# Moving the second weight matrix by eight words in both slots of an expert kernel

## The reference

```python
x = x + 0.5 * ffn(layernorm(x), Wr, W1, W3, W2)
x = x + attn(layernorm(x), Wq, Wk, Wv, Wc, Ltri)
x = x + 0.5 * ffn(layernorm(x), Wr, W1, W3, W2)
```

```python
h  = silu(xe @ W1[e]) * (xe @ W3[e])     # [tokens,256] x [256,1024], twice
ye = h @ W2[e]                           # [tokens,1024] x [1024,256]
out[token] += gate * ye
```

## The kernel before, in words

| what | address before | mod 64, mod 512 |
|---|---|---|
| slot A (`c_wa`), W1 high | 29184 | 0, 0 |
| slot A, W1 low | 53760 | 0, 0 |
| slot A, W2 high and low | 45568, 70144 | 0, 0 |
| slot B (`e_wb`), W1 high | 108064 | 32, 32 |
| slot B, W1 low | 132640 | 32, 32 |
| slot B, W2 high and low | 124448, 149024 | 32, 32 |
| `xT` high and low, `h` high and low | 157440, 161536, 173824, 190208 | 0, 256 |

## Time and profile before

### The profile page before, as it was taken

The page is one execution under the profiler, slowest core; times in us unless marked ns, Lnnn a source line. Parts: engine busy times, 40 slices in busy tenths (PEclk is TensorE's granted clock), DMA queues, the critical chain, the costliest instruction groups (busy, mean ns, idle before and its releaser), DMA issues.

```text
span 2968.2 us, 54854 instructions
## 1 busy us (share of the span) xinstructions
PE 2831.0 (95%) x18723; PEld 2535.6 (85%) x18723; DVE 1606.7 (54%) x3765; ACT 1305.6 (44%) x2765; POOL 1164.9 (39%) x1550
## 2 busy tenths in 40 slices
PE   4499999999999999989999995999999999999999
PEld 3389899989999989878888885998999998899988
DVE  8754545455454545447878875444545454545453
ACT  5543434444344434334444444444434343444443
POOL 3754434444444434310111113453444443444533
PEclk8799999999999999999999997999999999999999
DMA  7552323232332312121121014223323231323212
GB/s 247 194 127 36 80 36 79 43 78 39 84 63 54 86 31 42 33 59 33 57 70 47 31 45 123 57 43 76 83 38 79 41 86 29 81 42 79 43 29 34
DMA packets 155114, 197.23 MB, mean 66 GB/s; under 512 B 15536, under 2 KB 127024, under 8 KB 154928
## 3 DMA queue, kind: packets, MB, share of 16 engines
q0 software_dynamic: 62688, 87.11, 17.9%
q1 hardware_dynamic: 81952, 97.30, 10.1%
q10 hardware_dynamic: 10288, 10.38, 1.0%
HBM read 124.32 MB, written 78.79 MB: 68 GB/s over the span
## 4 chain that ended last, share of the span: by engine, by line
PE 54%; DVE 1%; ACT 0%; issue 0%; DMA 0%; POOL 0%; DVEq 0%; ACTq 0%; POOLq 0%
PE e_ps L100 8%; PE e_ps L102 8%; PE e_ps L101 8%; PE e_psy L1198 5%; PE mi_qk L1453 4%; PE e_ps L1198 3%; PE e_psy L1200 3%; PE mi_sc L1469 2%; PE mi_yo L1489 2%; PE mi_xv L1459 2%; PE mi_yo L1516 2%; PE e_ps L1200 2%; PE mi_kv L1503 1%; PE e_psx L1184 1%; PE mi_yo L1477 1%; PE mi_qk L1510 0%
## 5 line engine op out<-in xcount | busy, mean ns | idle before, releaser
L1301 DVE TENSOR_TENSOR e_h_lo<-e_hid,e_h_hi 128x384 fp32r<-128x384 f32 (+1 forms) x640 | 384.2, 600 | 399.3 <-ACT e_h_hi L1262 390.4
L1298 DVE TENSOR_TENSOR e_hid<-e_ps,e_gate 128x384 f32<-128x384 f32 (+1 forms) x640 | 381.9, 597 | 371.8 <-ACT e_gate L1258 357.3
L1262 ACT ACTIVATE e_h_hi<-e_hid 128x384 fp32r<-128x384 f32 (+1 forms) x640 | 356.9, 558 | 424.1 <-DVE e_hid L1298 417.0
L1258 ACT ACTIVATE e_gate<-e_ps 128x384 f32<-128x384 f32 (+1 forms) x640 | 333.8, 522 | 405.3 <-PE e_ps L102 397.9
L100 PE MATMUL e_ps<-e_xT_hi,e_wb 128*128 128x384 f32 (+1 forms) x1280 | 456.3, 357 | 0.0
L101 PE MATMUL e_ps<-e_xT_lo,e_wb 128*128 128x384 f32 (+1 forms) x1280 | 455.0, 355 | 0.0
L102 PE MATMUL e_ps<-e_xT_hi,e_wb 128*128 128x384 f32 (+1 forms) x1280 | 454.9, 355 | 0.0
L100 PE MATMUL e_ps<-e_xT_hi,c_wa 128*128 128x384 f32 (+1 forms) x1280 | 450.5, 352 | 2.5 <-DVE e_xT_lo L1290 2.5
L102 PE MATMUL e_ps<-e_xT_hi,c_wa 128*128 128x384 f32 (+1 forms) x1280 | 448.6, 350 | 0.0
L101 PE MATMUL e_ps<-e_xT_lo,c_wa 128*128 128x384 f32 (+1 forms) x1280 | 448.5, 350 | 0.0
L461 POOL DMA_INDIRECT c_xrow<-normed_rows,e_token x320 | 346.6, 1083 | 153.2 <-POOL e_token L1087 77.9
(11 more groups left out here) (302 smaller groups left out, 4772.3 us busy)
## 6 DMA issues: line engine op xcount, KB each, us to landing
c_raw<-w SPq DMA_DIRECT2D x204, 256.0 KB
normed_rows<-r_xn SPq DMA_DIRECT2D x8, 1056.0 KB, 7.1
normed_rows<-mi_xn SPq DMA_DIRECT2D x8, 1056.0 KB, 4.8
x<-x ACTq DMA_DIRECT2D x8, 1024.0 KB, 12.0
out<-mi_x SPq DMA_DIRECT2D x8, 1024.0 KB, 5.3
r_xin<-x SPq DMA_DIRECT2D x7, 1024.0 KB, 11.0
c_raw<-x SPq DMA_DIRECT2D x7, 1024.0 KB, 8.3
c_xrow<-normed_rows,e_token POOLq DMA_INDIRECT x320
```

The costliest lines, as they stand in the source:

```text
L1258: act.activation(gate[:, f % 2, 0:n], ps1[f % 2][:, 0:n], ACT.Silu).then_inc(gated, 1)
L1262: act.activation(h[0][:, f, 0:n], hid[:, f % 2, 0:n], ACT.Copy).then_inc(h_high, 1)
L1298: dve.tensor_tensor(hid[:, f % 2, 0:n], ps3[f % 2][:, 0:n], gate[:, f % 2, 0:n], ALU.mult).then_inc(hid_ready, 1)
L1301: dve.tensor_tensor(h[1][:, f, 0:n], hid[:, f % 2, 0:n], h[0][:, f, 0:n].bitcast(F32), ALU.subtract).then_inc(h_ready, 1)
```

## The change

Each part of a slot is widened from 6144 to 6160 words (`SPLIT`), and W2's columns begin at 4104 (`W2SPLIT`) in place of 4096. `split_piece` replaces `piece` wherever a piece is written to a slot or read back from it for the low part; the unsplit weights (`raw`) keep their layout. Slot B gets a spacer of 8 words ahead of it and one of 56 words behind it.

```diff
+SHIFT = 8
+W2SPLIT = W2AT + SHIFT
+SPLIT = WCOLS + 2 * SHIFT
...
+def split_piece(t, q):
+
+    at = q * PIECE + (SHIFT if q * PIECE >= W2AT else 0)
+    return t[:, at:at + PIECE]
...
-                    act.activation(piece(slot_a[:, 0], q), piece(raw, q), ACT.Copy).then_inc(w_high, 1)
+                    act.activation(split_piece(slot_a[:, 0], q), piece(raw, q), ACT.Copy).then_inc(w_high, 1)
...
-        slot_b = m.sb("wb", [P, 2, WCOLS], F32R)
+        m.sb("wb_shift", [P, SHIFT])
+        slot_b = m.sb("wb", [P, 2, SPLIT], F32R)
+        m.sb("wb_rest", [P, 7 * SHIFT])
...
-                        at = W2AT + f * D
+                        at = W2SPLIT + f * D
...
-        slot_a = m.sb("wa", [P, 2, WCOLS], F32R)
+        slot_a = m.sb("wa", [P, 2, SPLIT], F32R)
```

More of the change, by code:

```diff
@@ L861, in low_w @@
                     dve.wait_ge(w_high, q + 1)
-                    dve.tensor_tensor(piece(slot_a[:, 1], q), piece(raw, q), piece(slot_a[:, 0], q).bitcast(F32),
+                    dve.tensor_tensor(split_piece(slot_a[:, 1], q), piece(raw, q), split_piece(slot_a[:, 0], q).bitcast(F32),
                                       ALU.subtract).then_inc(w_low, 1)
@@ L908, in _ @@
                             pool.wait_ge(w_high, q + 1)
-                            pool.tensor_tensor(piece(slot_a[:, 1], q), piece(raw, q), piece(slot_a[:, 0], q).bitcast(F32),
+                            pool.tensor_tensor(split_piece(slot_a[:, 1], q), piece(raw, q), split_piece(slot_a[:, 0], q).bitcast(F32),
                                                ALU.subtract).then_inc(w_low, 1)
@@ L1243, in high_w @@
                     wait_raw(act, raw_loaded, e + loaded - 1, q)
-                    act.activation(piece(slots[1 - s][:, 0], q), piece(raw, q), ACT.Copy).then_inc(w_high, 1)
+                    act.activation(split_piece(slots[1 - s][:, 0], q), piece(raw, q), ACT.Copy).then_inc(w_high, 1)
                 def high_x(n, width=WIDE):
@@ L1283, in low_w @@
                     dve.wait_ge(w_high, PIECES * e + q + 1)
-                    dve.tensor_tensor(piece(slots[1 - s][:, 1], q), piece(raw, q), piece(slots[1 - s][:, 0], q).bitcast(F32),
+                    dve.tensor_tensor(split_piece(slots[1 - s][:, 1], q), piece(raw, q), split_piece(slots[1 - s][:, 0], q).bitcast(F32),
                                       ALU.subtract).then_inc(w_low, 1)
```

## The result

The changed kernel takes 2973.50 us (median of 22 runs, 2970.73 to 2975.44) against 2970.06 us of the kernel before in the same rounds (22 runs, 2968.18 to 2973.40). The ratio is 1.0013, 95% interval 1.0007 to 1.0019: slower by 3.4 us, where 13.8 us less had been forecast. The profiled execution has a span of 2971.5 us, 3.3 us more than before.

The account below looks back on a forecast made before the run. TensorE's distance from one matmul's start to the next was taken to bound both expert stages. Savings of 6.2 + 7.6 = 13.8 us, other items 0, took 2971.63 to 2957.8 us; range 2953 to 2973.

Parts of the forecast that it names:

- Items 4, 5 and 6: Slot writes at new remainders, earlier need for gathers, attention tensors moved by 128 bytes: each taken as costing nothing.
- Parts 1 and 2: Slot A's second product takes slot B's price, 6.2 us less; slot B's first product takes slot A's, 7.6 us less.
- No change: Rival: the slots' memory region makes their difference, so the change leaves both as they are; 2971.6 us, chance 0.13.
- Only one of the two: Rival: price depends also on history, so only one part's gain arrives; about 2965 us, chance 0.16.
- item 3: Slot A's W1 and slot B's W2 keep remainders modulo 64: 0 us, bounded by +31 and -31 us.
- item 6: Attention stage: its own tensors move by 128 bytes against constants that stay; taken as 0 us.
- The slower rival: 64 bytes between high and low part make slot A's 512 first and slot B's second products dear; +12.5 us, chance 0.15.

Follow-up runs that it names:

- e3: Kernel before with W2 moved 8 words in slot A only, high and low part at the same remainder: 2962.80 against 2970.00 us, ratio 0.9978.
- e4: Kernel before with only slot B changed, W1 at 0 and W2 at 32 modulo 512, no gap: 2961.75 against 2970.00 us, ratio 0.9973.
- e1: Kernel before with W1 at 0 and W2 at 32 modulo 512 in both slots, no gap between high and low part: 2954.98 against 2970.00 us, ratio 0.9950.
- e10: Changed kernel with slot B's start at 0 modulo 512 in place of 192, 64-byte gap kept: 2969.54 us, ratio 1.0000 to the kernel before.
- e5: e1 with slot B's start at 192 modulo 512, still no gap: 2962.48 us, ratio 0.9976 to the kernel before.
- e11: e1 with both slots starting at 64 modulo 512, xT and h unmoved: 2987.28 us, ratio 1.0058 to the kernel before.
- e12: e11 with xT, gate, hid and h moved by the same 64 bytes: 2955.50 us, ratio 0.9952 to the kernel before.
- e8: e1 with xT moved 8 words, to 32 modulo 64: 2969.47 us, ratio 0.9998 to the kernel before.
- e7: e1 with W2 16 words (64 bytes) behind its old place: 2968.26 us, ratio 0.9996 to the kernel before.

## Why the prediction was wrong

**The bound held.** TensorE's matmul distances set the end in both expert stages, before and after, and nothing became late: the waits have not grown and the attention has not changed. Items 4, 5 and 6 (writes, gathers, attention), costed at nothing, were right.

**Parts 1 and 2 were right in mechanism and size, taken by themselves.** 6.2 and 7.6 us had been forecast; e3 and e4 measured 7.2 and 8.3 us, and e1 15.0 us for both against 13.8. The excess of about 1 us is a price better than either slot had: the first product of 512 tokens takes 21.78 us in both slots of e1 where 21.83 had been forecast, 24 x 0.05 = 1.2 us. "No change" by the region of the memory falls with them: in e3 and e4 a slot takes the other's price without leaving its region. "Only one of the two" falls too, since the two add.

**The step that failed is item 3**, "0 us, if 64 bytes is the length that counts". Put at 0, it measured about +17 us: the changed kernel is 3.4 us slower where the other items gave 13.8 us less. The length is 256 bytes for the gap, and the change moves two things within it: the low part against the high part by 64 bytes, and slot B's start from 32 to 192, not to 0. Both slots being "at 0 modulo 64" was true and meant little. What they cost, in the step's own terms:

- The gap costs 15 us (e1 against e10). In the mean durations it sits on the product with the low part and the one before it (397 and 392 ns against 389).
- Slot B's start at 192 costs 7.5 us when there is no gap (e1 against e5). With the gap it costs less: 4 us by the medians of the runs (changed kernel against e10, with intervals that overlap), 2 us by the tile times summed over the two profiles: against e10, the second product in slot B loses 2.8 us and its 384 first product 1.1 us, and its 512 first product gains 2.3 us. The addresses agree with this smaller price: with a length of 256 bytes, the change puts slot B's low part back at 0 (256 modulo 512), and it is the high part that lies off, by -64. Its 512 first product, 22.02 us, is nearer to e5's 21.99 than to e10's 22.19. The tensors that item 6 speaks of moved by 128 bytes in the changed kernel and not in e10; no run tries that alone, and the attention, where it would show too, has not changed.

So -15 us for the two parts, +15 for the gap and +2 to +4 for slot B's start give about the +3.4 us measured. The upper bound that item 3 gave to itself, +31 us, was wide enough. The choice of 0, "which is where both slots agree for the 384 tiles although their addresses differ", used two remainders, 0 and 32, as if they stood for all. The remainders that the change makes new (64, 192, 224) had no row.

**The slower rival had the mechanism and not the price.** It named the 64 bytes between high and low part, and asked for L102's successor to split from the other two, which it does (397 against 389 ns). It had given +12.5 us, on the assumption that the dear price would replace each good one and that nothing would be gained. In fact the gain of the second product in slot A stayed whole, and a 384 first product, which had no dear price before outside an expert's first tile, got one (16.81 and 16.86 us). Its argument against itself, that two known prices leave no room for a third, was empty: 16.96 us in most 384 tiles (e11), 21.99 (e5) and 11.30 us (e11) are third prices.

**The range** ended at 2973 because the slower case had been left out as the two in ten; the measured 2973.5 lies 0.5 us above it.

**The rule** of the Trainium skill (SBUF — State Buffer, section "Who interferes with whom"), that the weights and the moving operand have independent read ports and that "PE and ACT never wait on anyone", was read as saying that placement changes nothing. These runs disagree with that reading: e11 and e12 have the same instructions and the same slots, and differ by 1.1% through the distance of the two operands. Not following it was right; no run shows what in the machine makes the difference, the ports or something else.

## What to carry to other kernels

Where TensorE is the bound and each matmul loads new weights, as in this kernel, the distance between the two operands' addresses can be worth half a percent (15 us of 2970 here). So, as far as this kernel shows, place all parts that take turns (high and low, the two slots) at the same remainder of 256 bytes, or of 512 to be safe, before trying where that remainder should be; being alike is not enough, as e11 shows, where all are alike at 64 and which is the slowest. A comparison of two placements shows the price of these two placements; for a change that makes a third, ask for every operand which remainder is new, and give that remainder a range of its own. A change of one offset that also alters a stride makes two changes, and the second should be padded away first.

## What the runs showed of the hardware

- The time from one start to the next, at the 1.00 clock, depends on how far the weights lie behind the other operand (`xT` or `h`); distances are here taken modulo 256 bytes, high and low part alike. For the first product the 96 matmuls of 512 columns take 21.78 us at a distance of 0 (e1), 22.39 at 32 and 22.39 at minus 32 bytes (before, e8), 22.40 at 64 (e11), 21.99 at minus 64 (e5). With 384 columns they take 16.65, 16.66, 16.64, 16.96 and 16.64 us (medians): the shorter matmul is less sensitive, but not free.
- For the second product the good distance is another: 8.41 us at 32 bytes, 8.55 at 0, 8.56 at 64, 8.49 at 96 and 8.56 at minus 32 (e1, before, e7, e11, e5).
- At the best distances tried, what is left looks like a fixed cost. The first product takes 226.9 ns for a matmul of 512 columns and 173.4 for one of 384 (21.78 and 16.65 us over 96). The difference, 53.5 ns for 128 columns, is close to one column for each period of 2.4 GHz (53.3 ns); above that 13.5 and 13.4 ns are left in each.
- The distance is not all: the same addresses can have two times. In the changed kernel 19 of the 27 second products of 384 tokens in slot B take about 8.55 us or more and the others 8.41. They go by position: in every expert the first 384 tile behind one of 512 takes 8.57 us, the next, where there is one, 8.41, the one after that 8.55. And e3, which moves W2 alone, takes slot A's first product with 512 columns from 21.83 to 21.78 us. So what ran just before has a part in the price, as with the odd tile in the earlier trace rows; how it does was not explained.
